# Gated stage: statistics, normalisation, key-value summary and residual shift at other places in the order, and one value-bias product in place of two

## The reference, cut to what matters

```
x = _ln(x, ln1_w, ln1_b)
qk = _silu(x @ Wqk.T + bqk)
v = _silu(x @ Wv.T + bv)
heads = qk[..., None, :] * gamma + beta
quad_q, lin_q, quad_k, lin_k = map(_rope, (quad_q, lin_q, quad_k, lin_k))
quad_att = jnp.einsum('bgid,bgjd->bgij', qq, qkk) / G + bias
attn = jax.nn.relu(quad_att) ** 2
quad_out = jnp.einsum('bgij,bgje->bgie', attn, vg)
lin_kv = jnp.einsum('bgnd,bgne->bde', lk, vg) / n
lin_out = jnp.einsum('bgnd,bde->bgne', lq, lin_kv)
gate = _silu(x @ Wg.T + bg)
out = gate * (qo + lo)
out = out @ Wo.T + bo
return _ln(out, ln2_w, ln2_b)
```

## Time and profile before

| what | value |
|---|---|
| runs | 1894.84, 1886.02, 1895.05 us; median 1894.84 |
| profiled execution, its own time | 1888.06 us |
| its span, first to last instruction | 1886.2 us |
| busy share of the span | PE 88%, PEld 61%, DVE 68%, ACT 55%, POOL 41% |
| mean granted TensorE clock | 0.959 |
| gated stage within the span | about 1396.9 to 1562.0 us |

### The profile page before, as it was taken

The page is one execution under the profiler, slowest core; times in us unless marked ns, Lnnn a source line. Parts: engine busy times, 40 slices in busy tenths (PEclk is TensorE's granted clock), DMA queues, the critical chain, the costliest instruction groups (busy, mean ns, idle before and its releaser), DMA issues. The chain is left out here.

```text
span 1886.2 us, 25944 instructions
## 1 busy us (share of the span) xinstructions
PE 1660.6 (88%) x8392; PEld 1159.0 (61%) x8392; DVE 1278.4 (68%) x3862; ACT 1028.4 (55%) x1734; POOL 769.6 (41%) x726
## 2 busy tenths in 40 slices
PE   3999679899898999895999789999969786999998
PEld 2777545455555555443777567777747664777776
DVE  4777567777777778743777567777645554766775
ACT  3665315565565566573666455555536534555554
POOL 3555501312311321111666546556552502555555
PEclk9999959999999999997999989999989997999999
DMA  4222111111111111100333231112100001121121
GB/s 135 95 94 90 47 32 32 19 23 21 22 28 24 22 30 19 24 6 28 114 120 115 68 113 54 46 46 85 51 0 1 1 1 45 66 81 52 57 71 37
DMA packets 58231, 95.03 MB, mean 50 GB/s; under 512 B 9312, under 2 KB 17120, under 8 KB 58096
## 3 DMA queue, kind: packets, MB, share of 16 engines
q1 hardware_dynamic: 55984, 91.07, 16.7%
q10 hardware_dynamic: 2112, 2.30, 0.4%
HBM read 76.76 MB, written 2.88 MB: 42 GB/s over the span
## 5 line engine op out<-in xcount | busy, mean ns | idle before, releaser
L923 ACT ACTIVATE att_probs<-banks 128x1024 f32<-128x1024 f32 (+3 forms) x384 | 306.2, 812 | 193.1 <-PE banks L834 191.0
L410 ACT ACTIVATE banks<-banks 128x512 f32<-128x512 f32 x384 | 223.8, 583 | 265.6 <-PE banks L323 261.1
L1048 DVE CUSTOM_DVE_ANT_0 banks<-banks,att_mask 128x128 f32<-128x128 f32 (+3 forms) x512 | 234.2, 523 | 69.5 <-PE banks L815 69.0
L815 PE MATMUL banks<-arena 128*128 128x512 f32 (+3 forms) x768 | 248.8, 405 | 28.1 <-DMA arena<-att_parts 15.7
L963 POOL TENSOR_SCALAR_AFFINE_SELECT att_probs<-att_probs 128x512 f32<-128x512 f32 x128 | 81.6, 637 | 418.7 <-ACT att_probs L923 418.7
L815 PEld LDWEIGHTS banks<-arena 128*128 128x128 f32 x768 | 132.7, 197 | 149.8 <-issue 90.3
L447 POOL TENSOR_TENSOR ffn1b_hid_l<-ffn1b_hid,ffn1b_hid_h 128x512 fp32r<-128x512 f32 x128 | 165.5, 1293 | 128.1 <-ACT ffn1b_hid_h L415 128.1
L447 POOL TENSOR_TENSOR ffn1a_hid_l<-ffn1a_hid,ffn1a_hid_h 128x512 fp32r<-128x512 f32 x128 | 165.9, 1296 | 123.2 <-ACT ffn1a_hid_h L415 123.2
L834 PE MATMUL banks<-arena 128*128 128x512 f32 (+3 forms) x768 | 204.2, 351 | 0.5 <-ACT att_probs L923 0.4
L1050 DVE TENSOR_REDUCE att_mx<-banks 128x1 f32<-128x512 f32 x256 | 162.1, 683 | 32.2 <-PE banks L815 32.0
L853 PE MATMUL banks<-att_probs,att_v_aug 128*32 128x512 f32 (+3 forms) x1536 | 165.5, 503 | 0.6 <-POOL att_probs L963 0.5
(11 more groups left out here) (386 smaller groups left out, 3763.9 us busy)
## 6 DMA issues: line engine op xcount, KB each, us to landing
ffn0a_share<-weight_rows SPq DMA_DIRECT2D x128, 128.0 KB, 3.0
ffn0b_share<-weight_rows SPq DMA_DIRECT2D x128, 128.0 KB, 3.0
ffn1a_share<-weight_rows SPq DMA_DIRECT2D x64, 256.0 KB, 4.1
ffn1b_share<-weight_rows SPq DMA_DIRECT2D x64, 256.0 KB, 4.0
arena<-att_parts SPq DMA_DIRECT2D x16, 384.0 KB
arena<-att_parts SPq DMA_DIRECT2D x128, 48.0 KB
w_raw<-in_ffn_w_dram SPq DMA_DIRECT2D x12, 256.0 KB, 3.1
out_dram<-x SPq DMA_DIRECT2D x8, 256.0 KB, 2.3
```

The costliest lines, as they stand in the source:

```text
L410: act.activation(gate if c < NSCALED else sil[:], gate, ACT.Silu).then_inc(silu_done, 1)
L815: mm = pe.matmul(bank[:, at:at + width], q_st[:, n % 3, t * P:(t + 1) * P], k_pad[:, n % 2, j, c * G:c * G + width], start=True, stop=True ...
L923: act.activation(probs[:, unit % NPROB, 2 * pair:2 * pair + 2, 0:c], score_ps[:, pair, :, 0:c], ACT.Exp, scale=SCALE).then_inc(exped, 1)
L1048: ins = dve.tensor_tensor_reduce(now, now, mask[:, G - width:G], 1.0, -3e38, ALU.add, ALU.max, best)
```

## The change

Four steps get other places in the order. `stats` and `norm` of batch b move from b-0.40 and b-0.38 to b-0.72 and b-0.71. `kv` of b moves from b+0.86 to b+1.02, so it stands behind both `ln` steps of b+1. `norm2` moves from b+1.73 to b+1.77, behind the `ktok` of b+1. The addition of `ln2b` into x leaves `norm` and becomes a step `shift` of its own on GpSimd at b+1.88; `sum` goes from b+1.80 to b+1.90.

Within a piece of `out`, the four `att` tiles now come first and the product with `kv`, with its wait for `kv_out`, last.

The value bias becomes one product per tile: the padded bias holds the row twice (rows 0 and 32). At the start of the stage ScalarE copies it into a rounded tile `bv`, and VectorE overwrites partitions 32 to 63 with the rest that rounding left off, so a single product with `ones` adds both. The bias leaves the pieces that ffn1a splits and joins those that it only loads. Two semaphores of the statistics become one (`moments`).

```
-            put(b - 0.40, "stats", b)
-            put(b - 0.38, "norm", b)
+            put(b - 0.72, "stats", b)
+            put(b - 0.71, "norm", b)
...
-            put(b + 0.86, "kv", b)
+            put(b + 1.02, "kv", b)
             put(b + 1.48, "tail", b)
-            put(b + 1.73, "norm2", b)
-            put(b + 1.80, "sum", b)
+            put(b + 1.77, "norm2", b)
+            put(b + 1.88, "shift", b)
+            put(b + 1.90, "sum", b)
...
+                pe.wait_ge(bv_split, 2)
...
-                    pe.matmul(to, ones[:], bv_h[:], start=False, stop=False)
-                    mm = pe.matmul(to, ones[:], bv_l[:], start=False, stop=True)
+                    mm = pe.matmul(to, ones[:], bv[:], start=False, stop=True)
...
             def out(b, c, h):
                 bank, full = fill(pe, "out", b, c, h)
+                pe.wait_ge(att_done, HALF * b + h + 1)
+                for t in range(TG):
+                    pe.matmul(bank[:, t * P:(t + 1) * P], v_tok[:, h * TG + t, c * P:(c + 1) * P],
+                              att[:, h, t * P:(t + 1) * P], start=t == 0, stop=False, skip_group_check=True)
                 pe.wait_ge(kv_out, b + 1)
...
+            act.activation(bv[:], bv_raw[:], ACT.Copy).then_inc(bv_split, 1)
...
+            def shift(b):
                 xs = k.x[:, b * S:(b + 1) * S].rearrange("p (t d) -> p t d", d=D)
-                pool.wait_ge(norm_done, b + 1)
                 pool.tensor_tensor(xs, xs, ln2b[:].unsqueeze(1).broadcast_to([P, NB, D]), ALU.add).then_inc(shifted, 1)
...
+            dve.wait_ge(bv_split, 1)
+            dve.tensor_tensor(bv[32:64, :], bv_raw[32:64, :], bv[32:64, :].bitcast(F32), ALU.subtract).then_inc(bv_split, 1)
```

More of the change, by code:

```diff
@@ L1155, in gated_tiles @@
     t.wvg_h, t.wvg_l = sb("wvg_h", [P, 2 * HV], F32R), sb("wvg_l", [P, 2 * HV], F32R)
-    t.bv_h, t.bv_l, t.ones = sb("bv_h", [P, HV], F32R), sb("bv_l", [P, HV], F32R), sb("ones", [P, P], F32R)
+    t.bv, t.bv_raw, t.ones = sb("bv", [P, HV], F32R), sb("bv_raw", [P, HV]), sb("ones", [P, P], F32R)
     t.wo_t, t.par, t.cols = sb("wo_t", [P, HV]), sb("par", [P, 10]), sb("cols", [P, 2 + EC])
@@ L1160, in gated_tiles @@
     t.pieces = [(a["gau_w"][:, 0:2 * P], t.wqk_h[:], t.wqk_l[:]),
-                (a["gau_w"][:, 2 * P:6 * P], t.wvg_h[:], t.wvg_l[:]),
-                (a["gau_bv"], t.bv_h[:], t.bv_l[:])]
-    t.plain = [(a["gau_w"][:, 6 * P:8 * P], t.wo_t[:]), (a["gau_par"], t.par[:]), (a["gau_cols"], t.cols[:]),
+                (a["gau_w"][:, 2 * P:6 * P], t.wvg_h[:], t.wvg_l[:])]
+    t.plain = [(a["gau_bv"], t.bv_raw[:]), (a["gau_w"][:, 6 * P:8 * P], t.wo_t[:]), (a["gau_par"], t.par[:]), (a["gau_cols"], t.cols[:]),
                (a["L1_attn_bo"].partition_broadcast(P), t.bo[:]), (a["L1_attn_ln2_w"].partition_broadcast(P), t.ln2w[:]),
@@ L1216, in sem @@
             return ctx.enter_context(nc.semaphore(f"gau_{name}"))
-        wqk_h, wqk_l, bv_h, bv_l, ones = own.wqk_h, own.wqk_l, own.bv_h, own.bv_l, own.ones
+        wqk_h, wqk_l, bv, bv_raw, ones = own.wqk_h, own.wqk_l, own.bv, own.bv_raw, own.ones
         wo_t, rel, angle = own.wo_t, own.rel, own.angle
@@ L1239, in phase_gated @@
         emptied = [sem(f"emptied{n}") for n in range(RING)]
-        stats_done, aggr_done, eps_done, rstd_done, norm_done = (sem(s) for s in
-            ("stats_done", "aggr_done", "eps_done", "rstd_done", "norm_done"))
+        moments, eps_done, rstd_done, norm_done = (sem(s) for s in ("moments", "eps_done", "rstd_done", "norm_done"))
+        bv_split = sem("bv_split")
         x_h_done, x_l_done, head_done, turn_done = sem("x_h_done"), sem("x_l_done"), sem("head_done"), sem("turn_done")
@@ L1338, in out @@
                 bank, full = fill(pe, "out", b, c, h)
+                pe.wait_ge(att_done, HALF * b + h + 1)
+                for t in range(TG):
+                    pe.matmul(bank[:, t * P:(t + 1) * P], v_tok[:, h * TG + t, c * P:(c + 1) * P],
+                              att[:, h, t * P:(t + 1) * P], start=t == 0, stop=False, skip_group_check=True)
                 pe.wait_ge(kv_out, b + 1)
[L1340 to L1346, removed]
+                pe.matmul(bank, kv[:, c * P:(c + 1) * P], turned[:, 1, h * G:(h + 1) * G], start=False, stop=True,
+                          skip_group_check=True).then_inc(full, 1)
             def ys(b, h):
@@ L1433, in tail @@
                 pool.tensor_tensor(nshift2[:], nmean2[:], rstd2[:], ALU.mult).then_inc(rstd2_done, 1)
-            walk(dict(norm=norm, tail=tail))
+            walk(dict(norm=norm, tail=tail, shift=shift))
         @block.vector
@@ L1442, in stats @@
                     ins = dve.bn_stats(st[:, t, :], k.x[:, b * S + t * P:b * S + (t + 1) * P])
-                ins.then_inc(stats_done, 1)
-                dve.wait_ge(stats_done, b + 1)
+                ins.then_inc(moments, 1)
+                dve.wait_ge(moments, 2 * b + 1)
                 pause(dve, k)
@@ L1447, in stats @@
                     ins = dve.bn_aggr(mv[:, t, :], st[:, t, :])
-                ins.then_inc(aggr_done, 1)
-                dve.wait_ge(aggr_done, b + 1)
+                ins.then_inc(moments, 1)
+                dve.wait_ge(moments, 2 * b + 2)
                 dve.tensor_scalar(veps[:], mv[:, :, 1], 1.0 + EPS, EPS * EPS, ALU.mult, ALU.add).then_inc(eps_done, 1)
@@ L1628, in laid_out @@
     bv = np.zeros((P, HV), get("L1_attn_bv").dtype)
-    bv[0] = get("L1_attn_bv")
+    bv[0], bv[32] = get("L1_attn_bv"), get("L1_attn_bv")
     made["gau_bv"] = bv
```

## The result

Four executions of the changed kernel took 1863.3 to 1868.1 us, median 1865.4, against 1891.9 for the kernel before, measured beside it. The ratio is 0.9864 with a 95% interval of 0.9831 to 0.9897. The profiled execution took 1867.24 us, its span 1865.4 us. The forecast was 1866 (1857 to 1880).

What follows compares the result with a forecast made beforehand. TensorE was taken to set the pace, losing time in its queue's waits. Batch 0 with the start 6.75, middle batches 11.6 and batch 3 6.4 make 24.75 us off 1891.0: 1866 us, range 1857 to 1880.

Steps and rivals of the forecast that it cites:

- Middle batches: Batches 1 and 2 of the gated stage: 28.6 instead of 34.44 us each, 5.8 us less, twice.
- new wait for `kv`: First output piece of batches 1 and 2: TensorE waits 0.6 us for ScalarE's copy of `kv`, out at +22.5.
- xn: GpSimd's eight tiles in a middle batch: 9 us, ready at +14.3, before TensorE asks at +16.6; the 2.38 us wait goes.
- Start: Ahead of the first statistics VectorE waits for ScalarE's bias copy, then subtracts: +0.55 us (0.3 to 0.9), all on the path.
- `proj` of batch 1: End of batch 0: the next `proj` at 1437.8 instead of 1444.55, 6.75 us less with the start counted in.
- Batch 3: Last batch: summary right behind the scores, output 6.93 us; +27.1 instead of +33.53, 6.4 us less.
- ffn1a: The stage that split the bias: GpSimd loses 0.75 us of work but stood idle 1.42 us, so no time changes.
- Value bias: In `v`, one product of five goes, eight in a batch; six count, 0.7 us, `v` ending at +13.95.
- Slow `xn`: Rival, chance 0.17: all eight `xn` tiles at 1.41 us beside the heads, the tail's power 2.2 us late; 1871 us.
- Both held: Rival, chance 0.12: VectorE's `turned` and GpSimd's `xn` exclude each other, 1.49 us per pair; 1877 us.
- The clock: Rival, chance 0.03: TensorE's granted clock drops to 0.50; two batches of it would give 1918 us.
- Little of it: Rival, chance 0.08: an unseen bank or buffer ties `xn`, `kv` or the layer norm to a later step; under 9.5 us, 1886.

Runs made afterwards that it cites:

- kv back: The changed kernel with the `kv` step back at b+0.86: 1868.3 us, ratio 0.9882; gated stage 140.1 us against 141.2 for the change.
- no swap: The changed kernel with the old order inside `out`, the `kv` product first and the four `att` tiles behind it: one execution of 1871.3 us, gated stage 144.4 us.
- shift in norm: The changed kernel with the addition of ln2b back at the end of `norm`, ahead of the tail on GpSimd: one execution of 1871.2 us, gated stage 144.0 us.
- the change again: The changed kernel itself measured once more, nothing edited, for the scatter: 1866.7 us, ratio 0.9883; gated stage 141.1 us.
- stats and norm early alone: The kernel before with only `stats` and `norm` moved to b-0.72 and b-0.71: 1885.6 us, ratio 0.9977; gated stage 160.9 us against 165.3.
- the run with two products: The changed kernel with the value bias as before, split in ffn1a and two products per tile: one execution of 1866.0 us, gated stage 141.8 us.
- both single edits: The kernel before with one edit each: `norm2` at b+1.77 (1888.5 us, ratio 0.9992), or `stats` and `norm` early (1885.6 us, ratio 0.9977).
- halves: The changed kernel with `xn` signalled by halves, second bias split behind the first statistics, `kv` at b+0.86 from batch 1 on: 1867.2 us, ratio 0.9881, stage 140.4 us.
- whole xn, y earlier, kv back: The changed kernel, no halves, `kv` at b+0.86 from batch 1, `y` at b+1.33 and b+1.37, second bias split later: 1866.9 us, ratio 0.9863, stage 136.0 us.
- both together: The kernel before with `stats` and `norm` early and `norm2` behind the key copies, nothing else: 1871.0 us, ratio 0.9907; gated stage 142.8 us.

## Why the prediction was right, point by point

*What bounds.* Right: TensorE's waits. Its busy time fell by 1.1 us in a middle batch, the period by 5.7 and 5.3 us.

*Middle batches.* Forecast 28.6 us, measured 28.75 and 29.09. The transposes and the summary wait for nothing, as said. The new wait for `kv` was forecast at 0.6 us and came at 0.51 and 0.85 us; "kv back" showed it as the price of that move, "no swap" showed the 0.9 us of cover, and "shift in norm" the 1.2 to 1.6 us a batch that the split-off shift saves. Taken away in "kv back", it gave 0.8 and 1.1 us. Part of the agreement is two errors that cancel. The chain to `kv` ran 0.4 us late in batch 1: y began at +10.71 instead of +10.25, the tail's power at +14.79 instead of +14.3, and `kv` was out at +22.88 instead of +22.5. Of that 0.3 us is the longer first step of `proj`. And the output behind the wait took 5.8 instead of 6.0 us, as it ends 0.3 us sooner with the `kv` product last. Batch 2 waits 0.34 us longer than batch 1 because VectorE began the statistics of y 0.45 us behind y there and 0.10 us in batch 1, so the tail's power came 0.34 us later; "the change again" shows the same. What held the statistics is open.

*xn.* Taken at 9 us between bounds of 6.25 and 11.3, measured 7.75 to 7.96 us. What I had left out is the power ahead of it: 2.03 us beside VectorE's products instead of 1.65. Together it was ready 0.6 us earlier than said (+13.7), and neither is on the path.

*Ends.* Start: forecast +0.55 us, measured +0.67 (0.21 us from the bias product to the statistics before, 0.88 after). The `proj` of batch 1: 6.75 us earlier, measured 7.0. Batch 3: 6.4 us less, measured 6.15. Both differences are mainly one term: the output with the next first start took 6.60 us instead of 6.93, which batch 0 gained, and the first step of `proj` took 0.32 us longer, which every batch behind it paid. Of batch 3's gain, 1.7 us is the summary at full clock, which "stats and norm early alone" had without any edit there; the forecast had it in through the 3.5 us. In ffn1a nothing: 319.9 us before, 321.3 after, and 321.5 to 321.7 in the four kernels that still split the bias there.

*Value bias.* 0.7 us a middle batch was the sum's term, on the path to v; the run with two products showed that none of it came out there, since the wait for `kv`, set by the tail, took it back. The sum took the later of the two times there, so the middle batches did not rest on the 0.7. Batch 3 did, and that run shows 0.7 us for it. In batch 0, where the forecast had ScalarE's key copies as the bound, they ended at 1432.40 and the summary began at 1432.50, as said; the run with two products shows that without the shorter `v` TensorE itself would have been 0.9 us later.

*The sum.* 24.75 us forecast for the stage, 24.2 measured. The last 0.6 us of agreement in the total is luck, since the rest of the kernel scatters by more.

*Rivals.* Slow `xn`: fell, 7.75 us. Both held: fell by this row of the changed kernel (durations ns min/median/max), 0.69 us for a head's product and 0.86 at most:

```profile
L1466 DVE TENSOR_TENSOR gau_turned<-gau_head,gau_angle x32: 680/693/858, 1420.5 to 1510.4; 128x512 f32<-128x512 f32 x32
```

The clock: 1.00 in each stretch read from batch 0's `gate` to the last `y`, so it did not decide here. But it did in both single edits, behind waits of 5.67 and 4.90 us. Little of it: fell.

## What to carry to other kernels

When an engine waits at two places in a loop for two different chains, removing one wait moves it to the other: here 1.3 us and 4.5 us alone, 22.6 us together. The wait that is left also grows, and a longer one can cost clock on top. So walk the loop with all edits in, not wait by wait, and ask of each chain when it ends rather than how long it makes others wait. A later step that a wait holds can be covered by putting the products that don't need it first; and an earlier start of TensorE is worth little if it then has to pause for the next half of its input.

## What the runs showed of the hardware

*Who holds whom.* GpSimd's two-input instruction held VectorE until it ended. In the changed kernel the shift ran from 1459.31 to 1461.68, and an `att` product that takes 0.69 us elsewhere ran from 1459.70 to 1462.22; in "stats and norm early alone" the shift ended at 1456.93 and a `nmean`, 0.17 us elsewhere, ran from 1455.22 to 1456.96.

```profile
1459.70 2.52 DVE L1476 SCALAR_TENSOR_TENSOR gau_att<-gau_att_s 128x512 f32<-128x512 f32 x1
```

GpSimd's tiles of `xn`, with one large input, hardly held VectorE's two-input products (`turned` took 0.68 to 0.86 us), but were held by them: up to 1.40 us instead of 0.79 in the changed kernel, as up to 1.41 in the earlier trace rows. The Trainium skill, SBUF — State Buffer, section "SBUF: two separate sides", has one lock that excludes both ways, for the whole instruction; a VectorE instruction with one input falls under it only in a mode that uses both ports. The shift agrees for `att`, which has two inputs (2.52 us); `nmean` (1.74 us) has one, and no view here shows its mode; `xn` agrees in one direction only.

*The clock.* Before, a wait of 3.06 us twice left the granted clock at 1.00, one of 3.07 us in batch 3 was followed by 0.69 over the summary, and one of 3.39 us by 0.50. In the runs, 4.90 and 5.67 us were followed by 0.50 and 0.57, 2.06 us by 1.00, and 3.05 us, at the place of the 3.07, by 1.00. So waits of the same length to 0.02 us were followed by different clocks, and the length alone does not tell which. In "halves", with a pause of 2.3 us ahead of `proj` and one in it, the clock stayed at 0.50 for 12 us from the first `proj`; in the changed kernel and in "whole xn, y earlier, kv back", with 1.4 us ahead and none in it, for about 5.

*Scatter.* The attention stage took 643.3 to 647.2 us in all but one of the profiled executions and 657.0 in that one, with no edit in it. There TensorE's busy time was 585.0 us at a granted clock of 0.93, against 571.1 us at 0.95 in the kernel before, with the same 3448 matmuls; these stretches are, first of "both together", then of the kernel before:

```profile
226.49:883.51 657.02, 585.04 (x3448) 329.83 (x3448) 463.07 (x1512) 352.65 (x481) 132.45 (x188) 0.93 0.12 22
```

The kernel before:

```profile
226.16:869.76 643.60, 571.11 (x3448) 325.42 (x3448) 462.51 (x1512) 352.67 (x481) 132.92 (x188) 0.95 0.12 22
```

So in that execution the longer stage goes with a lower clock; what lowered it I don't know.
